# Two sums of a scanned Mamba-style layer are written back into their PSUM banks, and the clip reads them there

## The reference

```python
xr, gate = split(x @ W_in.T, 2);  xr = xr + t_emb
xc = silu(causal depthwise conv of 4 taps(xr) + b_conv)
xn = (xc - mean) / sqrt(var + 1e-5) * ln_g + ln_b
Bm, Cm, dt = split(xn @ W_xproj.T, 3)            # 16 columns each
dt = tanh(dt @ W_dt.T + b_dt) * 0.01
Ad = 1.0 + dt * (-tanh(A_log))
Bd = Bm * minimum(norm(xn), 1.0)
def step(h, (ad, bd, xt, ct)):                   # h is [16 states, 1024 channels]
    h = clip(h * ad[:, None] + bd[:, None] * xt[None, :], -10, 10)
    return h, einsum('d,dh->h', ct, h)
y = scan(step) + D * xn
out = x + (y * silu(gate)) @ W_out.T
```

## Time and profile before

| | us |
|---|---|
| median of 3 runs (2164.7 to 2167.35) | 2166.88 |
| the profiled execution, its own time | 2165.86 |
| its span, from the first instruction to the last | 2164.1 |
| TensorE busy (16850 matmuls) | 1949.7, 90% |
| VectorE busy (2144 instructions) | 1774.6, 82% |
| GpSimd busy (1412) | 1769.2, 82% |
| ScalarE busy (3462) | 1434.0, 66% |
| mean granted TensorE clock | 0.987 of full speed |

### The profile page before, as it was taken

One profiled execution on the slowest core, in us unless ns is written; L12 is line 12 of the kernel. 1 busy time (PEld: TensorE's weight loads), 2 busy tenths in 40 slices (PEclk: granted clock), 3 DMA queues, 4 the chain that ended last, 5 costly groups with the idle time before them and its releaser, 6 DMA issues.

```text
span 2164.1 us, 46979 instructions
## 1 busy us (share of the span) xinstructions
PE 1949.7 (90%) x16850; PEld 1432.7 (66%) x16850; DVE 1774.6 (82%) x2144; ACT 1434.0 (66%) x3462; POOL 1769.2 (82%) x1412
## 2 busy tenths in 40 slices
PE   5789999999999999999999999999999999999987
PEld 5466666666666666666666666666666666666654
DVE  3488888888888888888888888888888888888896
ACT  4677766767766767766767766767766767766743
POOL 1398888888888888888888888888888888888886
PEclk8699999999999999999999999999999999999999
DMA  5122121112121112121112121112121112121110
GB/s 169 54 57 58 45 59 43 56 56 58 44 59 43 56 55 59 44 59 43 55 56 58 44 59 43 56 56 59 44 59 43 56 55 59 44 59 43 51 50 15
DMA packets 81992, 118.07 MB, mean 55 GB/s; under 512 B 21840, under 2 KB 50896, under 8 KB 77088
## 3 DMA queue, kind: packets, MB, share of 16 engines
q1 hardware_dynamic: 81760, 115.07, 18.6%
HBM read 59.96 MB, written 9.18 MB: 32 GB/s over the span
## 4 chain that ended last, share of the span: by engine, by line
PE 47%; issue 19%; DVE 13%; ACT 11%; POOL 9%; DVEq 0%; DMA 0%; POOLq 0%; SPq 0%; ACTq 0%
PE ps_job L450 8%; PE ps_y L571 7%; POOL prod L1076 7%; PE ps_job L455 7%; PE ps_fill L554 6%; PE ps_fill L545 4%; ACT low L765 4%; DVE h L927 4%; DVE ks L980 3%; PE ps_y L561 3%; PE ps_job L496 2%; PE ps_job L462 2%; PE ps_job L477 2%; ACT tap L725 2%; PE ps_job L486 2%
## 5 line engine op out<-in xcount | busy, mean ns | idle before, releaser
L1076 POOL TENSOR_TENSOR prod<-ks,crep 128x512 f32<-128x512 f32 x1024 | 1301.0, 1283 | 290.4 <-PE ps_y L571 249.9
L980 DVE TENSOR_TENSOR_SCAN ks<-low,ps_fill 128x512 f32<-128x512 f32 x1024 | 1222.5, 1207 | 218.1 <-PE ps_fill L554 213.3
L765 ACT COPY low<-ps_fill 128x512 f32<-128x512 f32 x1024 | 593.3, 579 | 578.4 <-PE ps_fill L545 569.1
L571 PE MATMUL ps_y<-c_sb,prod 128*128 128x128 f32 x4096 | 621.2, 274 | 0.7 <-POOL prod L1076 0.6
L571 PEld LDWEIGHTS ps_y<-c_sb,prod 128*128 128x128 f32 x4096 | 463.4, 141 | 95.5 <-issue 33.9
L554 PE MATMUL ps_fill<-spans,pick 128*128 128x512 f16 x1024 | 392.4, 383 | 97.3 <-ACT low L765 95.1
L545 PEld LDWEIGHTS ps_fill<-ts,xs 128*128 128x128 f16 x4096 | 314.2, 98 | 145.5 <-issue 3.3
L545 PE MATMUL ps_fill<-ts,xs 128*128 128x128 f16 x4096 | 396.9, 219 | 1.0 <-DMA xs<-h 1.0
L725 ACT ACTIVATE tap<-xr,cols_sb 128x128 f32<-128x128 f32 x768 | 251.7, 392 | 0.1
L450 PE MATMUL ps_job<-x,w_in 128*128 128x128 f16 x3072 | 215.3, 221 | 27.5 <-issue 19.8
L554 PEld LDWEIGHTS ps_fill<-spans,pick 128*128 128x128 f16 x1024 | 99.3, 97 | 203.2 <-ACT low L765 164.4
(11 more groups left out here) (126 smaller groups left out, 2254.1 us busy)
## 6 DMA issues: line engine op xcount, KB each, us to landing
crep<-c_dram SPq DMA_DIRECT2D x32, 1024.0 KB, 4.8
xs<-xh SPq DMA_DIRECT2D x256, 64.0 KB, 2.0
xs<-xl SPq DMA_DIRECT2D x224, 64.0 KB, 2.0
xf<-in_xT SPq DMA_DIRECT2D x32, 256.0 KB, 2.9
res<-in_x SPq DMA_DIRECT2D x32, 256.0 KB, 2.7
out_dram<-res SPq DMA_DIRECT2D x32, 256.0 KB, 2.1
ts<-tth SPq DMA_DIRECT2D x128, 32.0 KB
ts<-tth SPq DMA_DIRECT2D x128, 31.0 KB
```

The source lines that it names most:

```text
L571: last = mm(ps_y[:, u // 4, cut], prod[:, s % HOLD, e, :], ident, start=False, stop=(u % 4 == 3 and q == 3 and e == QN - 1), is_transpose= ...
L765: copy(low[:, s % RING], ps_fill[:, s % RING]).then_inc(sem["low_copied"], 1)
L980: nc.vector.tensor_tensor_scan(ks[:, u % 2, QN * q:QN * (q + 1)].rearrange("d n t -> d (n t)"), low[:, s % RING], ps_fill[:, s % RING], 0. ...
L1076: tt(prod[:, i % HOLD], ks[:, u % 2, part], crep[:, p, part], ALU.mult).then_inc(sem["weighed"], 1)
```

## The change

The first sum of z and the sum of a chunk's first step go back into the PSUM bank from which their input came, where they used to go to SBUF. The op that follows reads the bank. The clip of the first step stands now right behind its sum, in two halves of 16x512, and its single 16x1024 instruction at point 28 is gone. `z_taken` and `h0_taken` are raised by the second op of each pair and not by the first, `z1` and `h1_done` are dropped, and hend 0 moves from point 5 to point 6, on PE and on DVE.

```diff
-        JOBS = [(1, 3, "z", 0, 1, 1, 1), (1, 4, "gate", 0, 0, 2, 0), (5, 1, "hend", 0, -1, 2, 1),
+        JOBS = [(1, 3, "z", 0, 1, 1, 1), (1, 4, "gate", 0, 0, 2, 0), (6, 1, "hend", 0, -1, 2, 1),
...
-        TAKE = {("z", 0): 4, ("gate", 0): 5, ("hend", 0): 5, ("hend", 1): 7, ("yT", 1): 10, ("gate", 1): 11,
+        TAKE = {("z", 0): 4, ("gate", 0): 5, ("hend", 0): 6, ("hend", 1): 7, ("yT", 1): 10, ("gate", 1): 11,
...
                 if point == TAKE["z", 0] and exists(k, 1):
                     dve.wait_ge(sem["z_ready"], j + 1)
+                    stt(bank("z")[:, 0:3 * NS], sums[:, 0, :], tiny[:, 2:3], bank("z")[:, 0:3 * NS], ALU.mult, ALU.add
+                        ).then_inc(sem["z0"], 1)
                     since(dve, "zT_ready", j)
                     since(dve, "h0_ready", 2 * j)
-                    stt(z[:], sums[:, 0, :], tiny[:, 2:3], bank("z")[:, 0:3 * NS], ALU.mult, ALU.add
+                    dve.wait_ge(sem["z0"], j + 1)
+                    stt(z[:], bank("z")[:, 0:3 * NS], tiny[:, 1:2], sums[:, 1, :], ALU.mult, ALU.add
                         ).then_inc(sem["z_taken"], 1)
-                if point == 6 and exists(k, 1):
-                    dve.wait_ge(sem["z_taken"], j + 1)
-                    stt(z[:], z[:], tiny[:, 1:2], sums[:, 1, :], ALU.mult, ALU.add).then_inc(sem["z1"], 1)
...
-                    if point != TAKE["h0", i] or not exists(k, 1):
+                    if point != TAKE["h0", i] or not exists(k, 1) or first_chunk(j):
                         continue
 
                     half = slice(i * BANK, (i + 1) * BANK)
                     dve.wait_ge(sem["h0_ready"], 2 * j + i + 1)
+                    dve.wait_ge(sem["hend_taken"], 2 * k)
+                    dve.wait_ge(sem["decay0"], j + 1)
+                    stt(bank("h0", i)[0:NS], h1[:, half], first_decay[:], bank("h0", i)[0:NS], ALU.mult, ALU.add
+                        ).then_inc(sem["h0_sum"], 1)
+                for i in range(2):
+                    if point != TAKE["h0", i] + 1 or not exists(k, 1):
+                        continue
+
+                    half = slice(i * BANK, (i + 1) * BANK)
                     if first_chunk(j):
+                        dve.wait_ge(sem["h0_ready"], 2 * j + i + 1)
                         since(dve, "h1_high", j)
                         since(dve, "h1_low", j)
-                        nc.vector.tensor_copy(h1[:, half], bank("h0", i)[0:NS]).then_inc(sem["h0_taken"], 1)
                     else:
-                        dve.wait_ge(sem["hend_taken"], 2 * k)
-                        dve.wait_ge(sem["decay0"], j + 1)
-                        stt(h1[:, half], h1[:, half], first_decay[:], bank("h0", i)[0:NS], ALU.mult, ALU.add
-                            ).then_inc(sem["h0_taken"], 1)
+                        dve.wait_ge(sem["h0_sum"], 2 * (j - BATCH) + i + 1)
+                    tsc(h1[:, half], bank("h0", i)[0:NS], CLIP, -CLIP, ALU.min, ALU.max
+                        ).then_inc(sem["h0_taken"], 1)
...
-                if point == 28 and exists(k, 1):
-                    dve.wait_ge(sem["h0_taken"], 2 * (j + 1))
-                    tsc(h1[:], h1[:], CLIP, -CLIP, ALU.min, ALU.max).then_inc(sem["h1_done"], 1)
```

More of the change, by code:

```diff
@@ L78 @@
 out_ready out_taken
-halo_saved conv_taken stats aggr rstd moments z1 zb ad scan_p recip weighted bound32 bound16 bound_all p_kept
+halo_saved conv_taken stats aggr rstd moments z0 zb ad scan_p recip weighted bound32 bound16 bound_all p_kept
 norm_in xa xg xn_done xh_done xl_done yT_high squares root nrm nb16 tt_done skip_set y_opened kend_done c_out c_in
-y_gated h1_done carry16
+y_gated h0_sum carry16
 h0_ready h0_taken h1_in0 h1_in1 decay0 h1_high h1_low
@@ L665, in side @@
                     act.wait_ge(sem["nrm"], k + 2)
-                    act.wait_ge(sem["z1"], k + 2)
+                    act.wait_ge(sem["z_taken"], k + 2)
                     act_fn(z[:, 0:NS], z[:, 0:NS], ACT.Identity, scale=tiny[:, 6:7]).then_inc(sem["zb"], 1)
@@ L706, in side @@
                 if point == 41 and exists(k, 1):
-                    act.wait_ge(sem["h1_done"], k + 2)
+                    act.wait_ge(sem["h0_taken"], 2 * (k + 2))
                     if exists(k, 0):
@@ L853, in side @@
                     dve.wait_ge(sem["aggr"], j2 + 1)
-                    since(dve, "z1", j2)
+                    since(dve, "z_taken", j2)
                     tsc(tiny[:, 0:1], mom[:, 1:2], EPS, None, ALU.add)
@@ L1024, in body @@
                         pool.wait_ge(sem["norm_in"], k + 3)
-                        since(pool, "z1", k + 2)
+                        since(pool, "z_taken", k + 2)
                         since(pool, "xa", k + 2)
```

## The result

| | before | changed |
|---|---|---|
| median of 6 runs, us | 2164.74 (2163.17 to 2167.35) | 2146.17 (2143.19 to 2147.68) |
| profiled execution, its own time | 2165.86 | 2143.19 |
| steady turn of the loop, us | 64.92 | 64.25 |

The ratio is 0.991 with a 95% interval of 0.9897 to 0.9923: 18.6 us by the medians, where 26.4 were forecast. The turn is the mean distance between the first ops on z of neighbouring turns, over 25 turns or more; 31 x 0.67 = 20.9 us lies inside the interval of the gain, 16.7 to 22.3 us. The two profiled executions are 22.7 us apart, because the changed one happens to be the fastest of its six.

What follows compares the result with a forecast made beforehand. No engine's busy share named the limit; the chain of waits ran over TensorE, VectorE, ScalarE and GpSimd. Carry 21.7 plus z 4.7 gave 26.4 us: profiled 2139.5, median 2140.5 us, range 2132 to 2147.

Steps and rivals of the forecast that it cites:

- z term: At hend 0: z_taken comes later but widen and fill go first, gate job 0.15 us earlier a turn, 4.7 us.
- carry term: At TensorE's carry 1: the wait for L951 goes, ScalarE's take passes on 0.70 us a turn, 21.7 us.
- Only waited-for time counts: On VectorE: a shorter instruction is worth only what TensorE, and behind it ScalarE, waits for it; carry 1 0.87 a turn.
- The clip's price: First step on VectorE: each 16x512 clip from PSUM takes 0.68 us, the sum writing to PSUM stays 0.73.
- rival 2: First-step sum takes 1.41 us reading and writing one bank, clip 1 delays nb; 10 us kept, 2157 us; 9%.
- lower bound: For a half clip's time: L927's own running time of 0.57 us for two halves, so 0.29 for one.
- The clip's cover: Both half clips fit VectorE's idle time before the scans of slots 12 and 14, cost 0; second has 0.1 to 0.2 spare.
- upper bound for z: At hend 0: at most the whole wait of 0.25 us a turn is won.
- 1 (all VectorE time): All VectorE time saved on L927 and L869 counts: 69 us, 2098 us; 3%.
- 3 (given back): Gain lost further on where GpSimd and ScalarE are full (1039 to 1056): within 0.2%, 2163 to 2171; 8%.
- 4 (the clip still stands behind GpSimd): Clip 1 ahead of nb still waits behind a GpSimd product because it writes SBUF: +11 us, 2178 us; 7%.

Runs made afterwards that it cites:

- z half alone: Kernel before plus only both z ops over the PSUM bank and hend 0 at point 6, L927 kept at point 28: 2167.57 us, ratio 1.0006.
- first-step half: Kernel before plus only the first-step sum back to PSUM and the clip in two halves, z and hend 0 as before: 2142.51 us, ratio 0.9895.
- the run without a clip: Kernel before plus the first-step edit, but no chunk clipped and the sum going to SBUF: 2143.44 us, ratio 0.9890 against the kernel before.
- waits-first run: Changed kernel with z's two older waits (zT, h0) put ahead of its first op: 2142.67 us, ratio 0.9892 against the kernel before.
- half clips from SBUF: Changed kernel with first-step sum and half clips in SBUF at the same points: 2151.54 us, ratio 0.9932 against the kernel before.
- hend 0 at 5: Changed kernel with hend 0 back at point 5 on TensorE and VectorE: 2159.07 us, ratio 0.9963 against the kernel before.
- clip moved: Kernel before with the whole 16x1024 SBUF clip moved from point 28 to 23, behind the second sum: 2145.84 us, ratio 0.9912.
- both kernels with z at 7: Hend 0 at 6, z's second op from SBUF behind hend 1 at 7; with PSUM half clips 2132.58 us (0.9844), with the moved SBUF clip 2133.43 us (0.9852).

## Why the prediction was right, and what was mis-sized

The main mechanism, TensorE's wait for carry 1 and ScalarE as the next limit, was right. The z term was 7 us too high and the carry term 1 us too low, so 26.4 became 20.9 by the turns. That the time still fell in the range owes 2.1 us to the lower median of the kernel before.

1. **Only waited-for time counts: right.** 68 us of VectorE time went, and 21 us of the run by the turns. The z half alone sheds 53 us and gains nothing, the first-step half sheds 15 and gains 23.
2. **The clip's price: right.** 0.68 forecast, 0.67 measured; 0.73 for the sum that writes its own bank, 0.74 measured, where turns would have made it up to 1.41. So rival 2 falls. L927's own running time was put too low (0.57, against 0.68 when it was moved), which only shifts the lower bound.
3. **The clip's cover: right by luck.** It covers the halves, as the run without a clip shows. But I had not asked what stands between the halves: the weighting fell behind GpSimd (0.41 to 1.22 us) and took all of the margin that I put at 0.1 to 0.2 us. nb started 0.07 us late by it, which the next widen had made up.
4. **The carry term: 0.70 forecast, 0.74 measured** (first-step half alone), 31 x 0.74 = 23. ScalarE's low of slot 19 was named as the next limit and is it: the take starts 0.47 us behind it.
5. **The z term was wrong: +0.15 forecast, -0.07 measured** (64.18 to 64.25), 31 x 0.22 = 7 us of the 26.4. In the step "1006.49 + 0.24 + 0.03 + 0.24 = 1007.00" the gap was 0.14, since three waits and not one stand between the two ops (the waits-first run gives 0.10 back), and the op took 0.27. So the gate job starts 2.37 us behind the start of the scan of slot 3, against 2.39 before: 0.02 won, not 0.15. The remaining 0.09 lies between there and xr. On GpSimd the span from product 4 to the small op behind the power was, before,

```profile
1012.60 1.27 POOL L1076 TENSOR_TENSOR prod<-ks,crep 128x512 f32<-128x512 f32 x1 [2.20 <-PE ps_y L571]
1013.83 1.00 POOL L1036 TENSOR_TENSOR tiny<-tiny,halfs 128x1 f32<-128x1 f32 x1
1014.91 0.19 POOL L1065 TENSOR_TENSOR idle<-halfs 128x1 f32<-128x1 f32 x1
```

2.31 us and is 2.42 in the changed kernel's rows above. The skip op of VectorE (L968, two inputs in SBUF) stands behind the product there and holds up the power; in the changed kernel it comes at the same moment as the product, 1002.45, and holds up the product. TensorE's xr comes 0.10 us behind the end of what follows on GpSimd (L1051). No kernel was made to test this by itself, but the other traces bear it out: where z goes over PSUM (changed, z half alone, half clips from SBUF, waits first, hend 0 at 5), the skip op has a mean of 705 to 718 ns and TensorE's idle time ahead of xr is 22.5 to 22.6 us in the whole run; where it does not (before, first-step half with and without clip, clip moved, and both kernels with z at 7), 1100 to 1149 ns and 19.7 to 20.1 us. The difference is 0.08 to 0.09 a turn.
6. **What was missed in the other direction.** The stall of hend 0 was worth 0.42 us a turn, not 0.25, if one frees the bank early and keeps the move to point 6. The forecast's upper bound for z was therefore too low as well. The change spends it on a later `z_taken`.
7. **The rivals.** 1 (all VectorE time), 3 (given back) and 4 (the clip still stands behind GpSimd) are refuted: by the z half, by the turn of 64.18, and by clips of 652 to 679 ns in all 64 cases. What rival 4 feared befell the weighting.

The rule of the Trainium skill, "VectorE: DVE Perf Modes", section "Why PSUM operands drop a tier", agrees with the trace: 0.67 us for 512 elements from PSUM, 0.39 to 0.42 for 512 from SBUF without a stall, and 0.68 for 1024 from SBUF. The section "Who interferes with whom" of the Trainium skill's page "SBUF — State Buffer" lets no VectorE op with at most one SBUF input, outside the two-port modes, compete with GpSimd. The trace agrees: of the half clips from PSUM none was above 679 ns, and the sums, with one input in SBUF and one in PSUM, had a mean of 740.

## What to carry to other kernels

In this kernel a VectorE op with two SBUF inputs (0.25 or 1.22 us), or a one-source fp32 op inside SBUF (0.68 or 2.65), cost several times its own time when it met GpSimd's products; before rewriting such an op over PSUM, look for a place where GpSimd waits for somebody. A move of 0.6 us pushed a neighbour of the same kind out of its gap here, so list all such ops behind the edit. And free a bank with the first op that reads it: TensorE's wait on it cost 0.42 us a turn here, where the idle row said 0.25. Last, busy time that an edit removes says little about its worth: 53 us of it were worth nothing, 15 us were worth 23.

## What the runs showed of the hardware

- The same in-place 16x1024 fp32 op took 2.65 us at one place of the turn and 0.68 at another, and the same 128x48 op 1.22 and 0.25. I had expected the type of the op to decide this, not its place.
- L927 was issued at 1033.37, during the product of 1033.21. With its own 0.68 us it began to run about 1035.34 (an estimate, 1036.02 - 0.68), so it passed GpSimd's next boundary (1034.44) and went in near the one after (1035.45), while a half clip went in between two products at once. Why one boundary serves and another doesn't stays open.
- Two more semaphore waits between two VectorE ops cost 0.10 us a turn (a gap of 0.14 instead of 0.03), though the semaphores had been raised in the turn before.
- Reading and writing the same PSUM bank in one VectorE op cost next to nothing: 740 ns against 734 for 16x512, 247 against 238 for 128x48.
